# One instruction pair moved from VectorE to ScalarE and one from VectorE to GpSimd, in the third stage of a four-stage kernel

## The reference

```
xn = layernorm(x) * ln_g + ln_b            # x is layernorm(the block's input)
x_ssm, z = split(xn @ W_in)
x_ssm = silu(causal_depthwise_conv(x_ssm, conv_w) + conv_b)      # 4 taps
dt = softplus(x_ssm @ dt_w + dt_b)
Bm, Cm = x_ssm @ B_w, x_ssm @ C_w          # 16 states
for t in time:                             # h: [channel, state]
    h = h * exp(dt[t] * A)[..., None] + (dt[t] * x_ssm[t])[..., None] * Bm[t]
    y[t] = sum over states of h * Cm[t]
out = x + ((y + x_ssm * D_param) * silu(z)) @ W_out
```

## Time and profile before

| | us |
|---|---|
| median of 3 runs (1067.37 to 1071.03) | 1067.92 |
| the profiled execution | 1070.93 |
| its span in the profile | 1069.1 |
| the third stage's steps, in the span | about 559 to 775 |
| VectorE busy, whole span | 683.1 (64%) |
| TensorE busy, whole span | 876.1 (82%) |
| ScalarE busy | 556.9 (52%) |
| GpSimd busy | 460.7 (43%) |

### The profile page before, as it was taken

One profiled execution on the slowest core, in us unless ns is written; L12 is line 12 of the kernel. 1 busy time (PEld: TensorE's weight loads), 2 busy tenths in 40 slices (PEclk: granted clock), 3 DMA queues, 4 the chain that ended last, 5 costly groups with the idle time before them and its releaser, 6 DMA issues. The chain is left out here.

```text
span 1069.1 us, 21886 instructions
## 1 busy us (share of the span) xinstructions
PE 876.1 (82%) x8256; PEld 721.9 (68%) x8256; DVE 683.1 (64%) x1966; ACT 556.9 (52%) x1049; POOL 460.7 (43%) x781
## 2 busy tenths in 40 slices
PE   1878777276999999998958778887669999999994
PEld 1767766265888888876745556665447878888783
DVE  3566665366588888865249999999965073370712
ACT  1434343133567667664657777778455263452630
POOL 1456565323255455434446777777660011020201
PEclk9855566555799989898878888778668999999997
DMA  9100000110000000000000000000000000000000
GB/s 311 37 12 13 15 10 17 40 50 1 2 2 2 2 2 2 2 2 1 1 1 1 1 1 1 1 1 2 1 0 1 1 1 21 1 20 1 11 11 20
DMA packets 22134, 16.55 MB, mean 15 GB/s; under 512 B 2576, under 2 KB 20376, under 8 KB 21792
## 3 DMA queue, kind: packets, MB, share of 16 engines
q1 hardware_dynamic: 17408, 8.39, 2.8%
q10 hardware_dynamic: 4640, 7.01, 1.8%
HBM read 11.20 MB, written 4.19 MB: 14 GB/s over the span
## 5 line engine op out<-in xcount | busy, mean ns | idle before, releaser
L118 POOL TENSOR_TENSOR d_ln_ve<-d_ln_mv,eps 128x4 f32<-128x4 f32 x16 | 3.2, 201 | 228.7 <-DVE d_ln_mv L112 228.7
L1319 PE MATMUL ps<-h_h,wh_l 128*128 128x512 f32 x256 | 99.7, 390 | 0.0
L1320 PE MATMUL ps<-h_l,wh_h 128*128 128x512 f32 x256 | 99.7, 390 | 0.0
L1318 PE MATMUL ps<-h_h,wh_h 128*128 128x512 f32 x256 | 99.7, 390 | 0.0
L1393 PE MATMUL ps<-w_e,he 128*128 128x128 f32 x512 | 87.7, 311 | 4.4 <-ACT he L676 4.0
L1331 PEld LDWEIGHTS ps<-mov,hbd 32*128 32x128 f32 x2048 | 85.2, 251 | 0.0
L1331 PE MATMUL ps<-mov,hbd 32*128 32x32 f32 (+1 forms) x2048 | 83.1, 325 | 0.0
L676 ACT ACTIVATE he<-ps,pp 128x256 f32<-128x256 f32 x128 | 59.5, 471 | 44.2 <-PE ps L1320 39.1
L1393 PEld LDWEIGHTS ps<-w_e,he 128*128 128x128 f32 x512 | 77.4, 222 | 7.0 <-ACT he L676 6.3
L1285 DVE TENSOR_TENSOR d_y<-ps,w_s 128x512 f32<-128x512 f32 x8 | 5.5, 691 | 103.0 <-PE ps L1711 103.0
L1251 DVE TENSOR_TENSOR h_l<-hid,h_h 128x512 fp32r<-128x512 f32 x64 | 48.5, 772 | 31.2 <-ACT h_h L883 30.3
(11 more groups left out here) (254 smaller groups left out, 2637.9 us busy)
## 6 DMA issues: line engine op xcount, KB each, us to landing
x<-in_x SPq DMA_DIRECT2D x16, 128.0 KB
w_h<-in_w_h ACTq DMA_DIRECT2D x2, 1024.0 KB, 7.8
x<-x SPq DMA_DIRECT2D x16, 128.0 KB, 1.8
xB<-x SPq DMA_DIRECT2D x32, 64.0 KB
out_x<-xB SPq DMA_DIRECT2D x32, 64.0 KB
w_m<-in_w_m ACTq DMA_DIRECT2D x3, 256.0 KB, 4.8
xB<-in_w_e ACTq DMA_DIRECT2D x1, 512.0 KB
w_e<-in_w_e ACTq DMA_DIRECT2D x1, 512.0 KB
```

The lines of the kernel that those rows point to most:

```text
L1318: pe.matmul(dst, a_h, b_h, start=start, stop=True, skip_group_check=True)
L1319: pe.matmul(dst, a_l, b_h, start=False, stop=True, skip_group_check=True)
L1320: return pe.matmul(dst, a_h, b_l, start=False, stop=True, skip_group_check=True)
```

## The change

`conv_input` moves from VectorE to ScalarE, to the head of its step, and there is computed as x * c_rs[1] + shift. For that GpSimd's `scales` makes both shifts at once (c_nm, 128x4), where it made one (128x2). For tiles 0 and 1 the function stands ahead of step_b(13) and step_b(14), on ScalarE where it was on VectorE. `carried` moves from VectorE to GpSimd, to the head of its step, writes a tile of its own (hd_in) and signals c_hd, for which VectorE's `states` now waits.

```diff
-        c_ve, c_rs = ([sb(f"{n}{k}", [P, 2, 2]) for k in range(4)] for n in ("c_ve", "c_rs"))
+        c_ve, c_rs, c_nm = ([sb(f"{n}{k}", [P, 2, 2]) for k in range(4)] for n in ("c_ve", "c_rs", "c_nm"))
-        hd = sb("hd", [P, DS, NB])
+        hd, hd_in = (sb(m, [P, DS, NB]) for m in ("hd", "hd_in"))
 # GpSimd, scales(t)
-                chain.link(pool.tensor_tensor(c_ln1.nm[m][:, :], c_ln1.mv[m][:, :, 0], c_rs[m][:, 0, :], ALU.mult))
-                pool.tensor_tensor(c_ln1.nm[m][:, :], c_ln1.nm[m][:, :], minus[:, 0:2], ALU.mult
-                                   ).then_inc(c_ln1.rstd_ready, 1)
+                chain.link(pool.tensor_tensor(c_nm[m][:, :, :], c_rs[m][:, :, :],
+                                              c_ln1.mv[m][:, :, 0].unsqueeze(1).to_broadcast([P, 2, 2]), ALU.mult))
+                pool.tensor_tensor(c_nm[m][:, :, :], c_nm[m][:, :, :], minus[:, 0:2].unsqueeze(1).to_broadcast([P, 2, 2]),
+                                   ALU.mult).then_inc(c_ln1.rstd_ready, 1)
+
+            def carried(t):
+                pool.wait_ge(S["c_dec"], t + 1)
+                if t >= 1:
+
+                    pool.wait_ge(S["c_hs"], t)
+                decay = dec[t % 2][:, 1, 0:NB, CH - 1].unsqueeze(1).to_broadcast([P, DS, NB])
+                pool.tensor_tensor(hd_in[:, :, :], hc[t % 2][:, :, 0:NB], decay, ALU.mult).then_inc(S["c_hd"], 1)
 # GpSimd, step_c(n, have)
                 if n == 0:
                     products(1)
+                if have(0):
+                    carried(n)
                 if have(-2):
                     c_ln2.rstd_and_shift(pool, chain, eps, half, minus, (n - 2) % 4, n - 1)
 # ScalarE
+            def conv_input(t):
+                m = t % 4
+                act.wait_ge(c_ln1.rstd_ready, t + 1)
+                for b in range(2):
+                    last = act.activation(c_xq[t % 2][:, b, :], xblk(xB, 2 * t, b), ACT.Identity, bias=c_nm[m][:, 1, b:b + 1],
+                                          scale=c_rs[m][:, 1, b:b + 1])
+                last.then_inc(S["c_xn_"], 1)
 # ScalarE, step_c(n, have)
                 if n == 0:
                     in_and_out(1)
+                if have(2):
+                    conv_input(n + 2)
                 if have(1):
                     parts_of_step(n + 1)
 # ScalarE, the loop over the second stage's steps
             for n in range(-6, NB + 1):
+                if NB - 3 <= n < NB - 1:
+                    conv_input(n - (NB - 3))
                 step_b(n, n % 4, within(n))
 # VectorE
-            def conv_input(t):
-                m = t % 4
-                dve.wait_ge(c_ln1.rstd_ready, t + 1)
-                for b in range(2):
-                    last = dve.tensor_scalar(c_xq[t % 2][:, b, :], xblk(xB, 2 * t, b), c_ln1.mv[m][:, b, 0:1],
-                                             c_rs[m][:, 1, b:b + 1], ALU.subtract, ALU.mult)
-                last.then_inc(S["c_xn_"], 1)
-            def carried(t):
-                if t == 0:
-                    dve.wait_ge(zero_ready, 3)
-                else:
-
-                    dve.wait_ge(S["c_hs"], t)
-                chain.link(dve.tensor_tensor(hd[:, :, :], hc[t % 2][:, :, 0:NB], decay(t, 0), ALU.mult))
 # VectorE, states(t)
                 dve.wait_ge(S["c_st_ps"], t + 1)
+                dve.wait_ge(S["c_hd"], t + 1)
+                decay = dec[l][:, 1, NB:NCH, CH - 1].unsqueeze(1).to_broadcast([P, DS, NB])
                 state = ps[:, STATE, :].rearrange("p (n c) -> p n c", c=NCH)
-                chain.link(dve.tensor_tensor(hc[l][:, :, NB:NCH], hd[:, :, :], state[:, :, 0:NB], ALU.add))
-                chain.link(dve.tensor_tensor(hd[:, :, :], hc[l][:, :, NB:NCH], decay(t, 1), ALU.mult))
+                chain.link(dve.tensor_tensor(hc[l][:, :, NB:NCH], hd_in[:, :, :], state[:, :, 0:NB], ALU.add))
+                chain.link(dve.tensor_tensor(hd[:, :, :], hc[l][:, :, NB:NCH], decay, ALU.mult))
 # VectorE, step_c(n, have)
-                if have(2):
-                    conv_input(n + 2)
                 if have(0):
                     decay_products(n)
...
-                if have(0):
-                    carried(n)
                 if have(-1):
                     residual(n - 1)
```

More of the change, by code:

```diff
@@ L333, in build @@
             c_dt_ c_dec c_bcT c_prod c_g1_ps c_term c_ys c_xd c_cbd c_wall c_wt_ps c_u c_yi1 c_bbd c_xr c_br_ps c_wendT c_st_ps
-            c_hs c_hct_ps c_hcT c_yi_ps c_y c_out_ps c_o_ c_x d_xn_ d_t_ps d_xh d_xl d_y_ps d_o_ d_x d_stored""".split()
+            c_hs c_hd c_hct_ps c_hcT c_yi_ps c_y c_out_ps c_o_ c_x d_xn_ d_t_ps d_xh d_xl d_y_ps d_o_ d_x d_stored""".split()
         S = {n: sem(n) for n in SEMS}
@@ L770, in normed @@
                 for b in range(2):
-                    last = act.activation(c_xn[m][:, b, :], xblk(xB, 2 * t, b), ACT.Identity, bias=c_ln1.nm[m][:, b:b + 1],
+                    last = act.activation(c_xn[m][:, b, :], xblk(xB, 2 * t, b), ACT.Identity, bias=c_nm[m][:, 0, b:b + 1],
                                           scale=c_rs[m][:, 0, b:b + 1])
                 last.then_inc(S["c_xr"], 1)
+            def conv_input(t):
[5 more added lines that the diff above has]
+                last.then_inc(S["c_xn_"], 1)
             def chunk_weights(t):
@@ L1169, in weighted_input @@
                                   xs[l][:, :].rearrange("p (c t) -> p c t", t=CH), ALU.mult).then_inc(S["c_u"], 1)
-            def decay(t, k):
-                return dec[t % 2][:, 1, NB * k:NB * k + NB, CH - 1].unsqueeze(1).to_broadcast([P, DS, NB])
-            def carried(t):
-                if t == 0:
-                    dve.wait_ge(zero_ready, 3)
-                else:
-                    dve.wait_ge(S["c_hs"], t)
-                chain.link(dve.tensor_tensor(hd[:, :, :], hc[t % 2][:, :, 0:NB], decay(t, 0), ALU.mult))
             def states(t):
@@ L1291, in _ @@
             for n in range(-6, NB + 1):
-                if NB - 3 <= n < NB - 1:
-                    conv_input(n - (NB - 3))
                 step_b(n, n % 4, within(n))
```

## The result

Measured side by side in one set of runs, the kernel before took 1068.57 us in the median and the changed kernel 1066.42 (1061.97 to 1068.23): a ratio of 0.9973, with 95% interval 0.9961 to 0.9986. That is 2.2 us, 0.2%: no change by the bound of half a per cent, where 7.7 us were forecast. A second set with a copy of the changed kernel gave the ratio 0.9972 (0.9958 to 0.9985).

The account below looks back on a forecast made before the run. VectorE was taken to set the third stage's pace, with TensorE close behind. The terms 4.2 + 1.5 + 0.8 + 2.1 - 0.9 = 7.7 us, against the median 1067.92, gave 1060.2, predicted as 1060; range 1049 to 1069.

Parts of the forecast that it names:

- B: Rival: TensorE takes over all twelve third-stage middle steps, 14.1 us each; 1066.8 us in total, no change; chance 0.18.
- Twelve middle steps: Third stage, 582.86 to 749.65 us: half shortened, half staying long, 162.6 against 166.79, 4.2 us gained.
- First step: Third stage, 569.46 to 582.86 us, clock 1.00: both moved parts count, 0.73 + 0.80 = 1.5 us gained.
- Step 14: Third-stage step to 762.80 us, without a convolution input: gains 0.8 us.
- Last step: Third-stage step to 774.92 us: gains nothing, since VectorE waited 0.51 us for TensorE after the carried product.
- Seam: Entry into the third stage: TensorE's 5.65 us wait for c_xq goes and VectorE saves work, 2.1 us gained.
- End of the second stage: Inputs of tiles 0 and 1 on ScalarE, the second right ahead of GELUs TensorE waits for: 0.9 us lost.
- contention: VectorE's decay products lengthened by GpSimd's SBUF work beside them: 0.15 us a step, between 0 and 0.36.
- price by the rule: By the skill's SBUF rule, the carried product on GpSimd could cost VectorE's decay products its whole 0.81 us each step.
- given back whole: The convolution input's 0.73 us off VectorE returns as a new wait of some 0.8 us for TensorE's L1560.
- kind 2 steps: Third-stage steps with the convolution at TensorE's lower clock level, 3.54 us: forecast to stay at 14.1 us.
- C's ring: Rival: TensorE's turn of the next input waits behind ScalarE, a ring of 14.45 us; 1075.7 us total; chance 0.10.

Follow-up runs that it names:

- e1: Changed kernel with the carried product put back on VectorE, so only the convolution's input moved: 1073.39 us, ratio 1.0043 to before.
- e3: Changed kernel with GpSimd's carried product one place later, behind the second normalisation's small instructions: 1060.08 us, ratio 0.9922 to before.
- e4: The changed kernel again, unaltered, for a second profile: 1065.81 us.
- e5: Kernel before with one unused tile of 128 bytes per partition where the changed kernel has its c_nm tiles: 1073.83 us, ratio 1.0048.
- e2: Kernel before with only the carried product moved to GpSimd: 1066.52 us, ratio 0.9973.
- e6: Changed kernel with c_nm in the room of unused layer norm tiles, so addresses are those of before: 1060.95 us, ratio 0.9929 to before.
- e10: e6 with the convolution's inputs of tiles 0 and 1 back on VectorE: 1059.62 us, ratio 0.9913 to before.
- e11: Kernel before with the fourth stage's hidden tiles at offsets 32, 64, 256 and 512 from a multiple of 1024 bytes: one execution, 1069.8 us.
- e8: e1 with the addresses of before, so only the convolution's input moved and no tiles shifted: 1067.74 us, ratio 0.9995 to before.
- e9: e6 with GpSimd's carried product made twice, the first time into an unused tile: 1069.48 us, ratio 0.9993 to before.
- e7: Changed kernel with both the later place of e3 and the addresses of e6: 1055.92 us, ratio 0.9878 to before.
- e12: e7 with the fourth stage's d_xh and d_xl tiles moved to multiples of 1024 bytes: 1054.97 us, ratio 0.9855 to before.

## Why the prediction was wrong, and where it was right

**The step that failed** is the price of the tiles. The prediction said: "The widened factor pair (c_nm) has as many instructions as before, of 128x4 where they were 128x2", counted it as nothing, and had no term behind the last hand-over. The instructions cost nothing that the profiles show. Their four new tiles, a term that the sum did not have, cost 4.6 us (behind the last hand-over 299.0 us in the mean of five profiles with the shift: after, e1, e3, e4, e5; 294.4 in seven without it: before, e2, e6 to e10). Without them (e6) the same change gains 7.3 us, between 6.1 and 9.0 by its interval, where the sum had 7.7. No rival was near it. B gives 1066.8 and the time was 1066.42, but by chance: TensorE did not take over the steps.

**The parts of the sum**, forecast and measured in the profiles of after, e4 and e6, against before (e5 and e11 have its code too and agree with it within 0.1 us in these stretches):

- Twelve middle steps: 4.2 forecast, 6.4, 5.0 and 5.5 gained.
- First step: 1.5, and 1.5 in all three. Step 14: 0.8, and 0.5 to 0.6.
- Last step: 0, and 0.6 lost. VectorE's decay products took 4.17 us in this step and take 4.76: that is the loss. The carried product, 1.01 us here, gave nothing back, as forecast: from VectorE's c_ya to the residual it is 2.3 us with and without it, by way of TensorE's output product, and the wait ahead of the residual went from 0.51 to 1.31 us.
- Seam: 2.1, and 1.5. TensorE's wait of 5.65 us for c_xq fell to 0.62, its turn is at 550.49 and no longer at 559.30 (some 4 us of this come from ahead of the change). But VectorE's decay products there take 3.71 us and took 2.92, 0.8 more, which the forecast did not have.
- End of the second stage: 0.9 lost forecast, 0.1 to 0.3 measured. TensorE's wait there grew from 1.74 to 2.51 us, but the stage's last three steps, seen on VectorE, went from 16.45 to 16.35, from 21.46 to 21.91 and from 18.12 to 17.92.

**The middle steps came out near by two errors against each other**, which is luck. First: contention was put at 0.15 us a step, at most 0.36, and the walls alone grew by 1.00. The product alone makes 0.85 of it (e2), the convolution's input alone 0.24 (e8). Two of the seven before, and after (by form, the twelve middle steps: busy us, mean ns):

```profile
L1105 DVE TENSOR_TENSOR wall<-dec,wall 128x96 f32<-128x96 f32 x12 | 3.5, 293 | 0.4
L1105 DVE TENSOR_TENSOR wall<-dec,wall 128x64 f32<-128x64 f32 x12 | 2.8, 231 | 0.4
```

after:

```profile
L1120 DVE TENSOR_TENSOR wall<-dec,wall 128x96 f32<-128x96 f32 x12 | 8.4, 702 | 0.4
...
L1120 DVE TENSOR_TENSOR wall<-dec,wall 128x64 f32<-128x64 f32 x12 | 7.5, 624 | 0.4
```

e3 shows that the place beside the walls is the cause (0.6 to 0.7 a step back), e9 that more of it costs more. The Trainium skill (SBUF — State Buffer, Who interferes with whom) says that a VectorE instruction with two SBUF inputs contends with a GpSimd instruction that reads SBUF. The trace agrees: the walls of 64 and 96 columns, which met the product, went from 231 and 293 ns to 624 and 702, and 0.22 became 0.67 in e9. The prediction had the price by the rule, the product's whole 0.81 us a step, and e2's 0.85 is that; e9's second product cost the walls only half its length. The smaller figure was taken since L1150 grew by 0.36 only, which is one instruction where there are seven walls. Second: VectorE was to wait about 0.8 us for L1560, now L1559. It waited for it only once, 1.0 us in the first step. The longer walls fill that time; the prediction had said so of the rule's price ("they have the 0.8 us of new wait to lose"), and should have used it. For the convolution's part alone "given back whole" is right: e8 gains nothing in the stage. And the kind 2 steps, which were to stay at 14.1 us, became steps of 13.2 to 13.9 in after. The forecast's own picture, shorter steps beside some of 14.1 in which the residual waits for TensorE's output product, appears only in e3, e7 and e12, where the product no longer meets the walls. TensorE's granted clock over the twelve steps was 0.88 and not 0.82; e9, with steps of 13.94, has 0.81. Which of the two follows the other, the runs don't say.

**Right, too:** VectorE set the pace; ScalarE's wait ahead of c_zb (8.9 us in twelve) went to 0.2; GpSimd's ahead of its sums from 20.6 to 12.7; C's ring did not close, c_xq never made TensorE wait by more than 0.8 us.

## What to carry to other kernels

A new tile is part of a change's cost: it moves every tile allocated behind it, and here 128 bytes in the third stage made a fourth stage that nobody had touched 4.6 us slower. List the addresses before and after, and compare the stretches that the diff does not touch first. And work moved from VectorE to GpSimd had its price here beside VectorE's instructions with two operands in SBUF (0.85 us for a product of 0.87), and none that shows beside those with one operand in PSUM (e3): look for such a place in GpSimd's order before counting the gain.

## What the runs showed that I had not expected

- The rate of a 128x512 matmul on the hidden tiles depends on where its streamed tile begins: 227 ns from start to start at multiples of 256 bytes (0, 256 and 512 tried), 229 at 64 (2.75 / 12), 233 at 32 and at 128, all at a granted clock of 1.00.
- VectorE's products with two operands in SBUF take 0.67 us with 32 columns, where 0.22 is their own time, if a 128x256 product of GpSimd runs beside them (e9); products with one operand in PSUM kept 1.21 and 0.68 us beside the same instruction (e3).
- Two parts that gain nothing (e8) and 2.1 us (e2) alone gain 7.3 together (e6). A reading, not tested by itself: the one opens the wait that the other's contention fills (ahead of c_yi VectorE waits 2.9 us in e8's middle steps and not at all in e6's).
